# Context attention: half projections in two passes of 64 rows, each beside one head's scores, and odd slots that begin with the weighing

## Reference

```
qh = (q @ Wq + bq).reshape(B, LQ, HEADS, D_K).transpose(0, 2, 1, 3)
kh = (k @ Wk + bk).reshape(B, LKV, HEADS, D_K).transpose(0, 2, 1, 3)
vh = (v @ Wv + bv).reshape(B, LKV, HEADS, D_K).transpose(0, 2, 1, 3)
scores = jnp.einsum('bhqd,bhkd->bhqk', qh, kh) * scale
attn = jax.nn.softmax(scores, axis=-1)
out = jnp.einsum('bhqk,bhkd->bhqd', attn, vh)
```

## Time and profile before

| | |
|---|---|
| median of 3 runs | 1417.14 us (1416.73 to 1419.59) |
| the profiled execution | 1416.92 us, of which its span 1415.1 us |
| slots 0 to 511 in the trace | 65.2 to 950.8 us |
| PE, DVE, ACT busy | 1357.3, 1071.3, 960.0 us |

### The profile page before, as it was taken

The page is one execution under the profiler, slowest core; times in us unless marked ns, Lnnn a source line. Parts: engine busy times, 40 slices in busy tenths (PEclk is TensorE's granted clock), DMA queues, the critical chain, the costliest instruction groups (busy, mean ns, idle before and its releaser), DMA issues.

```text
span 1415.1 us, 32674 instructions
## 1 busy us (share of the span) xinstructions
PE 1357.3 (96%) x13282; PEld 793.4 (56%) x13282; DVE 1071.3 (76%) x2114; ACT 960.0 (68%) x1997; POOL 287.2 (20%) x321
## 2 busy tenths in 40 slices
PE   7799999999999999999999999899999999989998
PEld 4244555444555444555444545457557999856666
DVE  4777787888787888787888888725876768767757
ACT  5367787877788777888777666753796654348731
POOL 3344222212212222212223000000003100001110
PEclk9799999999999999999999999998999999999999
DMA  6846454345454345454345522001402320356000
GB/s 177 190 135 160 118 138 110 75 115 137 107 139 111 71 119 137 105 138 114 70 109 160 131 46 46 2 15 47 120 24 64 110 66 1 93 122 147 1 1 30
DMA packets 98791, 134.55 MB, mean 95 GB/s; under 512 B 11024, under 2 KB 74128, under 8 KB 92688
## 3 DMA queue, kind: packets, MB, share of 16 engines
q1 hardware_dynamic: 98640, 132.45, 37.4%
HBM read 94.15 MB, written 38.27 MB: 94 GB/s over the span
## 4 chain that ended last, share of the span: by engine, by line
PE 86%; DVE 7%; ACT 5%; issue 1%; DMA 1%; SPq 0%; POOL 0%; ACTq 0%; DVEq 0%; POOLq 0%
PE psum L553 19%; PE psum L573 17%; PE psum L534 7%; PE psum L606 4%; PE psum L2182 4%; PE psum L2156 3%; PE psum L653 3%; PE psum L1276 2%; PE psum L2901 2%; DVE peaks L714 2%; ACT probs L812 2%; PE psum L613 2%; PE psum L1673 1%; PE psum L275 1%; PE psum L2911 1%; PE psum L2864 1%
## 5 line engine op out<-in xcount | busy, mean ns | idle before, releaser
L714 DVE TENSOR_REDUCE peaks<-psum 128x1 f32<-128x512 f32 x1024 | 656.1, 686 | 157.5 <-PE psum L534 147.7
L812 ACT ACTIVATE probs<-psum 128x512 f32<-128x512 f32 x1024 | 556.3, 596 | 181.0 <-PE psum L553 170.2
L553 PE MATMUL psum<-queriesT,keysT 64*128 64x256 bf16 (+1 forms) x4096 | 332.6, 274 | 16.6 <-ACT probs L812 16.1
L553 PEld LDWEIGHTS psum<-queriesT,keysT 64*128 64x128 bf16 (+1 forms) x4096 | 166.3, 95 | 210.7 <-ACT probs L812 167.2
L573 PE MATMUL psum<-probs,values 128*17 128x256 f32 x4096 | 271.7, 383 | 0.0
L534 PE MATMUL psum<-keysT,queriesT 64*128 64x512 bf16 x1024 | 211.1, 381 | 8.6 <-DMA keysT<-key_parts 4.9
L573 PEld LDWEIGHTS psum<-probs,values 128*17 128x17 f32 x4096 | 94.2, 96 | 128.0 <-issue 77.8
L962 POOL CAST key_parts<-key_f 128x512 bf16<-128x512 f32 x57 | 34.7, 609 | 494.9 <-ACT key_f L851 452.0
L534 PEld LDWEIGHTS psum<-keysT,queriesT 64*128 64x128 bf16 x1024 | 59.9, 95 | 31.5 <-DVE peaks L714 18.9
L606 PE MATMUL psum<-ctxT,wk 128*128 128x256 f32 x192 | 67.1, 431 | 0.2 <-DVE peaks L714 0.2
L968 POOL TENSOR_TENSOR key_parts<-key_r,key_parts 128x512 bf16<-128x512 f32 x57 | 65.9, 1157 | 4.6
(11 more groups left out here) (321 smaller groups left out, 1739.3 us busy)
## 6 DMA issues: line engine op xcount, KB each, us to landing
keysT<-key_parts SPq DMA_DIRECT2D x186, 256.0 KB, 5.8
key_parts<-key_parts SPq DMA_DIRECT2D x90, 256.0 KB
ctx_nat<-in_ctx_dram SPq DMA_DIRECT2D x32, 256.0 KB, 3.2
ctx_in<-in_ctx_dram SPq DMA_DIRECT2D x24, 256.0 KB, 4.7
ctx_turned<-ctxT SPq DMA_DIRECT2D x24, 256.0 KB, 6.2
ctx_T<-ctx_turned SPq DMA_DIRECT2D x12, 512.0 KB, 4.0
qk_parts<-early_weights SPq DMA_DIRECT2D x24, 128.0 KB
q_parts<-q_parts SPq DMA_DIRECT2D x20, 128.0 KB
```

What stands on the lines that cost most here:

```text
L553: made = e.matmul(ps[j][:, e2 * S:(e2 + 1) * S], self.keysT[own, plane, i % RING, kt * P:(kt + 1) * P], self.queriesT[own, plane, u % 2, g ...
L714: e.tensor_reduce(self.peaks[:, i % 2, j * QT + qt, c:c + 1], k.ps(("max", n)), AX.X, ALU.max).then_inc(*self.peaked.up(n))
L812: e.activation(self.probs[:, t % RINGP, 2 * j * S:(2 * j + 2) * S], k.ps(("scores", t, j)), ACT.Exp).then_inc(*self.exped.up((t, j)))
```

## The change

Four things change. **(1)** Every *fill half* and every value projection from batch 1 on (now always *make half*; the double *make values* is left to batch 0) is made as two matmuls that accumulate in one bank: rows 0 to 63 of the contraction, then rows 64 to 127. Both are in the 64-row tile mode. The first stands beside the scores of head 1, the second beside those of head 0. **(2)** An even slot with such a job is: first half, four scores of one head, two maxima, two scores of the other head, second half, its last two scores. An even slot without one keeps the alternating scores. **(3)** An odd slot begins with the weighing and its jobs and ends with scores and maxima, which are staggered so that one head's scores end early. ScalarE and VectorE follow: in odd slots jobs first, then exponentials or maxima. The heads' order alternates from slot to slot (`order`). **(4)** The plan: 192 half jobs stand one in each even slot from 18 to 408 but 22, 24, 402 and 404; the preparation of the queries moves from odd slots up to 25 into even slots up to 16; the context is turned 16 slots earlier; normalize moves from slot 16i+20 to 16i+21. Waits for the context buffer are by chunk now.

```diff
+def order(t):
+
+    return (0, 1) if t % 2 else (1, 0)
...
-            at(6 * b, "norm x", b)
-            at(6 * b + 3, "scale x", b)
-            at(6 * b + 5, "turn x", b)
-            at(6 * b + 7, "make queries", b)
+            at(4 * b - 2, "norm x", b)
+            at(4 * b, "scale x", b)
+            at(4 * b + 2, "turn x", b)
+            at(4 * b + 4, "make queries", b)
...
-                    at(slot, "turn ctx", b, c)
+                    at(slot - 16, "turn ctx", b, c)
...
-                at(SLOTS * i + SLOTS + 4, "normalize", i)
+                at(SLOTS * i + SLOTS + 5, "normalize", i)
...
+                for e2 in range(2):
+                    at(SLOTS * NG * b - 110 + 8 * p + 2 * e2, "make half", b, p, e2)
...
+        def score(t, j, *steps):
...
+            if steps[0] == 0:
+                banks.use((2 * t + order(t).index(j)) % HALVES, w, ("scores", t, j), (self.exped, (t, j)))
...
+        def half_job(t, part, job, *a):
+
+            own = slice(part * HALF, (part + 1) * HALF)
...
+            if part == 0:
+                misc(t, name, (kept, done))
+                w.wait_ge(*self.ctx_turned(b, c))
+                e.matmul(k.ps(name)[:, 0:S], stationary, moving, start=True, stop=False).then_inc(
+                    *self.half_made.up((job,) + tuple(a)))
+            else:
+                w.wait_ge(self.half_made, (job,) + tuple(a))
+                e.matmul(k.ps(name)[:, 0:S], stationary, moving, start=False, stop=True).then_inc(*made_by.up(done))
...
+        def even_slot(t, maxima):
...
+            if not halves:
+                both_scores(t)
+                for n in maxima:
+                    find_max(n, t)
+                return
+            half, = halves
+            early, late = order(t)
+            half_job(t, 0, *half)
+            score(t, early, 0, 1, 2, 3)
+            for n in maxima:
+                find_max(n, t)
+            score(t, late, 0, 1)
+            half_job(t, 1, *half)
+            score(t, late, 2, 3)
+
+        def odd_slot(t, maxima):
...
+            first = maxima[0]
+            score(t, early, 0)
+            find_max(first + late, t)
+            score(t, early, 1, 2)
+            score(t, late, 0)
+            score(t, early, 3)
+            score(t, late, 1)
+            find_max(first + early, t)
+            score(t, late, 2, 3)
...
+            elif t % 2:
+                weigh(t)
+                jobs(t)
+                odd_slot(t, maxima)
+            else:
+                even_slot(t, maxima)
+                jobs(t)
```

More of the change, by code:

```diff
@@ L463, in plan @@
         at(STREAM_STARTS[1] + 32, "stream", "next turn", 0)
+        for jobs in due.values():
+            jobs.sort(key=lambda job: job[0] not in HALF_JOBS)
         return due
@@ new lines, in score @@
+        def score(t, j, *steps):
+            i, p = divmod(t, SLOTS)
+            u, g = divmod(i, UNIT_GROUPS)
+            if steps[0] == 0:
+                banks.use((2 * t + order(t).index(j)) % HALVES, w, ("scores", t, j), (self.exped, (t, j)))
+            ps = k.ps(("scores", t, j))
+            for step in steps:
+                e2, plane = divmod(step, 2)
+                kt, own = 2 * p + e2, slice(j * HALF, j * HALF + (TALL if plane == REST else HALF))
+                made = e.matmul(ps[:, e2 * S:(e2 + 1) * S], self.keysT[own, plane, i % RING, kt * P:(kt + 1) * P],
+                                self.queriesT[own, plane, u % 2, g, :], start=(plane == MAIN), stop=(plane == REST))
+            if step == 3:
+                made.then_inc(*self.scored[j].up((t, j)))
@@ new lines, in weigh @@
+        def weigh(t):
+            if not BLOCK + 1 <= t <= TOTAL + 1:
+                return
+            i, p0 = divmod(t - BLOCK - 1, SLOTS)
+            b, g = divmod(i, NG)
+            w.wait_ge(self.exped, (t - 2, order(t)[1]))
+            for p in range(p0, p0 + BLOCK):
+                w.wait_ge(self.v_kept, (b, p))
+            w.wait_ge(self.ones_set, b % 2)
+            if i:
+                w.wait_ge(self.outT_kept, i - 1)
+            w.wait_ge(self.cleared, 0)
+            for p in range(p0, p0 + BLOCK):
+                for e2 in range(2):
+                    for j in range(GH):
+                        quad, half, kt = e2 * GH + j, 2 * j + e2, 2 * p + e2
+                        made = e.matmul(k.bank(SUMS)[32 * quad:32 * quad + DH + 1, 0:S],
+                                        self.values[b % 2][:, kt, g * GH + j, :],
+                                        self.probs[:, (SLOTS * i + p) % RINGP, half * S:(half + 1) * S],
+                                        start=(p == 0), stop=(p == SLOTS - 1))
+            made.then_inc(*self.weighed.up((t - BLOCK - 1) // BLOCK))
@@ new lines, in even_slot @@
+        def even_slot(t, maxima):
+            halves = [job for job in self.due.get(t, ()) if job[0] in HALF_JOBS]
+            w.wait_ge(self.shiftT_kept, t // SLOTS)
+            w.wait_ge(self.ones_in, 0)
+            if not halves:
+                both_scores(t)
+                for n in maxima:
+                    find_max(n, t)
+                return
+            half, = halves
+            early, late = order(t)
+            half_job(t, 0, *half)
+            score(t, early, 0, 1, 2, 3)
@@ new lines, in even_slot @@
+            score(t, late, 0, 1)
+            half_job(t, 1, *half)
+            score(t, late, 2, 3)
+        def odd_slot(t, maxima):
+            early, late = order(t)
+            if not maxima:
+                both_scores(t)
+                return
+            first = maxima[0]
[7 more added lines that the diff above has]
+            score(t, late, 2, 3)
@@ L728, in peak, with jobs @@
                 *self.shift_found.up(("rest", i)))
-        for t in range(FIRST, TOTAL + 3):
-            for n in self.maxima(t):
-                peak(n)
+        def jobs(t):
             for job, *a in self.due.get(t, ()):
@@ L771, in vector @@
                     k.stream.vector_job(e, w, *a)
+        for t in range(FIRST, TOTAL + 3):
+            if 0 <= t < TOTAL and t % 2:
+                jobs(t)
+                for n in reversed(self.maxima(t)):
+                    peak(n)
+            else:
+                for n in self.maxima(t):
+                    peak(n)
+                jobs(t)
     def scale_heads(self, e, w, i):
@@ L798, in scalar, with exponentials @@
         k = self.k
-        for t in range(FIRST, TOTAL + 3):
+        def exponentials(t):
             if 0 <= t < TOTAL:
@@ L809, in scalar @@
                     w.wait_ge(self.split_dve, ("part2", "q"))
-                for j in range(GH):
+                for j in order(t):
                     w.wait_ge(self.scored[j], (t, j))
@@ L903, in scalar @@
                     k.stream.scalar_job(e, w, *a)
+        for t in range(FIRST, TOTAL + 3):
+            if t % 2:
+                keep_sums(t)
+                jobs(t)
+                exponentials(t)
+            else:
+                exponentials(t)
+                jobs(t)
     def pool_chunks(self):
@@ L948, in gpsimd @@
                     inverse(QT * a[0])
-                elif job == "make values" and a == [1, 0]:
+                elif job == "make half" and a == [1, 0, 0]:
                     w.wait_ge(self.q_made, B - 1)
```

106 lines of the change are left out of this document (40 added, 66 removed).

## The result

The changed kernel takes 1394.18 us (median of 4 runs, 1393.13 to 1396.79). The kernel before, run beside it, takes 1416.93 (4 runs, 1415.45 to 1419.59). The ratio is 0.984, with a 95% interval of 0.982 to 0.986: 23 us faster, where 33 were forecast. The profiled execution of the changed kernel took 1394.46 us.

What follows compares the result with a forecast made beforehand. TensorE, busy 96% of the span, was taken as the bound, with holes behind exponentials in even slots without a job. Terms -48 + 9.5 - 5.4 + 5 + 6 = -33 took 1416.92 to 1384 us; range 1362 to 1412.

Steps and rivals of the forecast that it cites:

- Term A: Even slots: half jobs in two 64-row passes overlap the scores, 82 us instead of 129.5, gain 48.
- Rivals 3 and 4: TensorE: strict start order, 1424, chance 0.12; no overlap of float32 with bf16, 1545, chance 0.05.
- Term E: Even slots: second pass waits for the first's semaphore with almost no slack; loss 6, bounds 0 and 19.
- rival 2: The rings bind: late head waits 0.10 longer per even slot because ScalarE is late; 1402, chance 0.17.
- Term B: Even slots without a half job: hole behind the odd slot's scores, waiting for an exponential; loss 9.5.
- Term C: 59 even slots with a 128-row job: job and weighing become one excursion from the tile mode; gain 5.4.
- Term D: Odd slots: VectorE normalizes ahead of the maxima, so a bank comes free late, 25 times; loss 5, bounds 0 and 10.
- The start: Slots 2 to 16: stall of the denser query preparation, unpriced, within a chance of 0.04 shared with slots 410 to 511.
- 12 us of waits outside my pieces: Pieces gave 873 us, trace 885; the difference, start (slots 0 to 4) and scattered VectorE waits, was assumed to stay.
- an even slot of 1.19: Sign in the changed trace: 1.19 us between the starts of an even slot and its weighing.
- a pair of 2.85: Sign in slots 30 to 400: a pair of slots takes 2.85 us, against 3.15 before.
- a middle some 46 us shorter: Sign in the changed trace: slots 26 to 409, 633 us before, some 46 shorter.

Runs made afterwards that it cites:

- free_order: Changed kernel with maxima and exponentials over half their columns, and the second pass ahead of all four late scores: 1370.35 us, ratio 0.968.
- half1_first: Changed kernel with the half job's second pass issued ahead of all four late scores instead of between them: 1394.79 us, ratio 0.987.
- shift_dve: Changed kernel with the second head's copy of the turned shift made by VectorE instead of ScalarE: 1389.42 us, ratio 0.981.
- outside: Changed kernel with the rotated order only for slots 16 to 411, the old order elsewhere: 1383.01 us, ratio 0.979.
- max_short: Changed kernel with VectorE's maxima reading 256 of the 512 columns: 1386.05 us, ratio 0.981.

## Why the forecast was right in sign and 10 us short

**Term A** (half jobs, -48). Confirmed in kind: a score starts within .01 us of 360 of the 384 first-pass matmuls and within .04 of the others. Rivals 3 and 4 are out: 1.40 and 2.06 were their marks for an even slot, and 1.27 was seen. By the Trainium skill's rule (page "TensorE: Matmul & The Clock Gate", section The mechanism, matmuls start and end in strict program order) the late score at 466.22 in free_order could not start ahead of the L586 at 466.23 that stands before it; in the timeline of PE of half1_first, where the pass stands first in the program too, the score is .08 ahead:

```profile
464.46 0.28 PE L551 MATMUL psum<-queriesT,keysT 64*128 64x256 bf16 x1
464.54 0.40 PE L586 MATMUL psum<-wv,ctxT 64*128 64x256 f32 x1
```

The traces disagree with the rule for tiles of different rows. In half1_first the late head's first score is ahead of the pass in 167 of 192 even slots. What runs ahead is only the matmul, though. The weight loads of the two keep the program's order in all 192, and here the score's load comes straight behind the pass's, which had waited for its semaphore:

```profile
464.45 0.18 PEld L586 LDWEIGHTS psum<-wv,ctxT 64*128 64x128 f32 x1
464.46 0.11 PEld L551 LDWEIGHTS psum<-queriesT,keysT 64*128 64x128 bf16 x2
```

So the tiles run at their own pace behind work that is issued, but not past a wait for a semaphore: in the earlier trace rows one score starts at 78.31, the next in the program waits for an exponential, and the rest of the first head's scores, on the other rows and waiting for nothing, start with it at 79.00. The two edits also need each other here: rotation without two passes is 1521, two passes in the old order 1420 at best (1542 with the banks in one round).

**Term E** (small waits, forecast +6, bounds 0 to 19) is the step that failed in size. I had named the wait (.215 + .38 + .05 = .65 against rows free at .66) and called it just covered. What I left out is the weight load behind it, which carries the wait itself: in none of the six kernels of the table does it start before .43. The second matmul of the second pass stands .32 behind that load, not .215, and the weighing .31 behind that. The late scores, whose loads stand among these, aren't the reason: the trace of before shows the same .32 at the place of the earlier trace rows, where float32 tiles of 32 rows start from an idle engine. The first load there starts at 1000.25 and its tile's second matmul at 1000.57, so the forecast could have had this price. The pair is 2.94, not 2.85: .09 × 186 = 17 us instead of 6, inside the bounds and inside rival 2's price, but by another mechanism than its rings.

**Not in the forecast**: the two pairs at a *turn shift*. The first pair of a group, whose half job waits for the copies of the shift, lost (.40 - .12) × 23 = 6.4 us; shift_dve got 6.3 back in slots 29 to 401. The pair before it, with the transposes themselves, gained (.37 - .07) × 24 = 7.2 us. Before, these transposes stood between the half job and the next scores and took .21 by themselves, and the second maximum behind them started .15 late, waiting for VectorE. Now the weighing starts among them, and that maximum is .08 late. First the timeline of PE before, then that of the changed kernel:

```profile
393.35 0.28 PE L641 MATMUL psum<-ident_b,shift_b 128*2 128x128 bf16 x4
393.56 0.62 PE L553 MATMUL psum<-queriesT,keysT 64*128 64x256 bf16 x8
```

```profile
381.35 0.22 PE L697 MATMUL psum<-ident_b,shift_b 128*2 128x128 bf16 x2
381.36 0.40 PE L605 MATMUL psum<-probs,values 128*17 128x256 f32 x2
381.40 0.22 PE L697 MATMUL psum<-ident_b,shift_b 128*2 128x128 bf16 x2
```

Together the two pairs cost .49 above two plain ones before and .47 now. Against the kernel before, then, the shift lost nothing, and what shift_dve gets back is a gain beyond it.

**Term B** (hole, +9.5): slots 401 to 509 lost 8.7 of the 9.5, and outside recovered all of it. Right in place and size.

**Term C** (modes, -5.4): in part wrong. I had counted a 128-row job and the weighing as one excursion. Two rows of the timeline of PE of before price a *turn ctx* (L590) by itself, .49 when the gathering, also a 128-row job, follows:

```profile
403.10 0.66 PE L590 MATMUL psum<-const,ctx_in 128*128 128x128 f32 x4
403.59 0.53 PE L674 MATMUL psum<-const,outT 128*128 128x34 f32 x4
404.05 0.62 PE L553 MATMUL psum<-queriesT,keysT 64*128 64x256 bf16 x8
```

After, a *turn ctx* pair costs .59 over a plain one: the .49 and a second change of mode of .10. That concerns 24 of the 59 slots, 2 us.

**Term D** (normalize, +5): 3.57 against 2.94, .63. The gathering itself takes .57 of TensorE's time in the odd slot (its L746 starts at 465.94, the next score at 466.51), against .46 before (403.59 to 404.05 above), and max_short shows that waits for VectorE are .07 of the .63. The term's size, .16 a time or 4 us, was met mostly for another reason.

**The start**: slots 3 to 29 took 2.6 us more, for the queries. I had given this .04 with no price.

Together these are 11 (E) + 2 (C) + 3 (start) + 6 - 7 (the two pairs of the shift) = 15 us worse than the sum, where the whole is 10 worse. The other 5 us, by subtraction, have no cause here, and the spread behind slot 509 is as large. I had assumed that 12 us of waits outside my pieces would stay. In the middle few of them were scattered: over slots 29 to 401 the pairs of before lie 3 us in all above the shortest of their kind. So part of the forecast's closeness is luck: at the shift a loss and a gain of the same size, neither in any term, made up for each other.

No run moved the first pass ahead of its wait (into the odd slot), which would test the .09 directly. That the wait and its load set it rests on the table, where nothing else moves it.

The marks that held: a score beside each first pass, the stretches where losses were forecast with their holes, and maxima in the middle that wait beyond .06 us only at normalize and shift. Those that didn't: an even slot of 1.19 (1.27 seen), a pair of 2.85 (2.94), and a middle some 46 us shorter (36 in slots 17 to 401).

## What to carry to other kernels

When several waits of some hundredths end together, none of them is shown to be the limit: take each load away in turn, and if the period doesn't move, look for the interval that stays the same in every variant. Two passes into one accumulator that are tied by a semaphore cost the flight of the first, the signal and an uncovered weight load, here .43 + .32 = .75 from the first pass's second matmul to the second pass's second, where .215 + .215 was the work. Leave that much room for it, with other work between. Rotate an order only in the stretch that needs it, since jobs that filled a hole elsewhere stop filling it.

## What was unexpected of the hardware

- A matmul whose rows are still busy doesn't hold back a later one of the other row half: the score at 464.46 started ahead of the pass at 464.54. One that waits for a semaphore does: in the earlier trace rows three scores on free rows stood from 78.31 to 79.00 behind the other head's wait, and in all 192 even slots of half1_first the weight loads keep the program's order.
- A float32 weight load of 64 rows takes .18 us. Hidden, its matmul lasts .37; exposed behind a wait, with its rows free (free_order), .46, and the next starts .30 behind instead of .215.
- A change from 128-row jobs to the weighing's narrow column tiles costs .10 us (four transposes of 128 rows took .59 at 77.15, where a 128-row job follows them they took .49), as the change from 64 rows to 128 does.
- Transposes that write two columns of the array don't hold the weighing's first matmuls back: 381.36 stands between 381.35 and 381.40. Before, with scores behind them, four of them took .21 of TensorE's time (393.35 to 393.56).
